# Turning the last query tile's attention probabilities on VectorE and by way of DRAM, for three heads of four, in the first layer

## What is computed

```
h = layernorm(x) * (1 + ca) + sa
q, k, v = h @ q_w, h @ k_w, h @ v_w            # 16 heads of 16 features
scores = q @ k.T / 4 - slope[head] * |i - j|   # per batch and head, 512 x 512
scores = where(j <= i, scores, -inf)
attn = softmax(scores, axis=-1)
x = x + ga * ((attn @ v) @ o_w)
```

## Time and profile before

| | us |
|---|---|
| median of 3 runs | 2975.95 |
| lowest and highest | 2972.04, 2979.3 |
| profiled execution | 2970.31 |
| its span | 2968.5 |
| TensorE, VectorE, ScalarE busy in the span | 2771.0, 1723.5, 1402.0 |

### The profile page before, as it was taken

The page is one execution under the profiler, slowest core; times in us unless marked ns, Lnnn a source line. Parts: engine busy times, 40 slices in busy tenths (PEclk is TensorE's granted clock), DMA queues, the critical chain, the costliest instruction groups (busy, mean ns, idle before and its releaser), DMA issues. The chain is left out here.

```text
span 2968.5 us, 51611 instructions
## 1 busy us (share of the span) xinstructions
PE 2771.0 (93%) x19492; PEld 1833.8 (62%) x19492; DVE 1723.5 (58%) x5077; ACT 1402.0 (47%) x3113; POOL 819.9 (28%) x829
## 2 busy tenths in 40 slices
PE   6889999888799999999999999999999787899998
PEld 3556666664456565656666665656566444478887
DVE  4667777767766565656565555656663688631113
ACT  3666676652445454554545454545442232232224
POOL 1001111113433333323232333333332210035551
PEclk8999999999899999999999999999999899899999
DMA  5111111002554545545555546454441000213325
GB/s 147 19 19 19 19 19 19 14 4 74 169 157 118 155 131 170 160 134 150 146 165 155 158 125 176 122 168 124 143 132 61 11 15 15 71 43 84 76 81 195
DMA packets 218343, 294.19 MB, mean 99 GB/s; under 512 B 23075, under 2 KB 155174, under 8 KB 213984
## 3 DMA queue, kind: packets, MB, share of 16 engines
q1 hardware_dynamic: 209264, 270.37, 31.5%
q0 software_dynamic: 7680, 16.32, 2.1%
q10 hardware_dynamic: 1152, 4.19, 0.4%
HBM read 159.45 MB, written 127.50 MB: 97 GB/s over the span
## 5 line engine op out<-in xcount | busy, mean ns | idle before, releaser
L1576 PE MATMUL bank<-w,gT 128*128 128x256 f32 x2048 | 478.7, 385 | 2.6 <-ACT gT L1494 2.6
L1543 PE MATMUL bank<-h2T,w 128*128 128x512 f32 x1024 | 452.7, 595 | 0.0
L1576 PEld LDWEIGHTS bank<-w,gT 128*128 128x128 f32 x2048 | 379.2, 190 | 90.5 <-issue 44.1
L1494 ACT ACTIVATE gT<-bank,vec 128x512 f32<-128x512 f32 x256 | 175.9, 687 | 425.4 <-PE bank L1543 425.4
L1543 PEld LDWEIGHTS bank<-h2T,w 128*128 128x128 f32 x1024 | 192.1, 190 | 219.6 <-issue 215.2
L609 ACT ACTIVATE y<-y,least 128x128 f32<-128x128 f32 (+3 forms) x512 | 252.0, 554 | 51.5 <-DVE least L479 51.5
L1166 POOL TENSOR_TENSOR prob<-prob,rsum 128x512 f32<-128x512 f32 (+1 forms) x256 | 232.0, 932 | 150.4 <-DVE rsum L1347 150.3
L479 DVE CUSTOM_DVE_ANT_0 y<-bank,mask 128x128 f32<-128x128 f32 (+3 forms) x512 | 223.9, 485 | 71.1 <-PE bank L706 70.2
L1438 ACT ACTIVATE prob<-prob,least 128x256 f32<-128x256 f32 (+1 forms) x512 | 238.2, 466 | 2.2 <-DVE least L1324 2.2
L1324 DVE CUSTOM_DVE_ANT_0 prob<-bank,mask 128x256 f32<-128x256 f32 (+1 forms) x512 | 164.3, 387 | 121.2 <-PE bank L1531 121.2
L1514 PE MATMUL bank<-wtok,hT 128*128 128x512 f32 x512 | 226.5, 595 | 1.3 <-ACT hT L1429 1.3
(11 more groups left out here) (326 smaller groups left out, 4834.6 us busy)
## 6 DMA issues: line engine op xcount, KB each, us to landing
turned_probs<-prob_blocks SPq DMA_DIRECT2D x128, 256.0 KB, 5.5
probT<-turned_probs SPq DMA_DIRECT2D x32, 1024.0 KB, 5.9
turned_rows<-score SPq DMA_DIRECT2D x252, 128.0 KB, 3.1
score<-turned_rows SPq DMA_DIRECT2D x63, 512.0 KB, 3.6
turned_probs<-prob_blocks SPq DMA_DIRECT2D x128, 192.0 KB, 3.1
probT<-turned_probs SPq DMA_DIRECT2D x32, 768.0 KB, 5.0
w<-in_W SPq DMA_DIRECT2D x8, 1024.0 KB, 8.1
turned_queries<-kneg SPq DMA_DIRECT2D x128, 64.0 KB
```

Of the source, the lines that this page charges most:

```text
L1494: nc.scalar.activation(gT[:, m, :], M[m % 2][:, :], ACT.Gelu, bias=vec[:, h // B, 4 * KD + m:4 * KD + m + 1])\
L1543: ins = nc.tensor.matmul(M[m % 2][:, :], w1[:, k, m * P:(m + 1) * P], h2T[:, k, :], start=(k == 0), stop=(k == KD - 1))
L1576: ins = nc.tensor.matmul(M[i][:, (t % 2) * D:(t % 2 + 1) * D], gT[:, m, t * P:(t + 1) * P], w2[:, m, :], start=(m == 0), stop=(m == MF - 1))
```

## The change

```diff
+            def move_wide(m):
+                sp.wait_ge(s["wide_turned"], ROUND * (m + 1))
+                if m:
+                    sp.wait_ge(s["wide_in"], 16 * m)
+                for i in range(GROUPS):
+                    src = blocks[SQUARE * i:SQUARE * (i + 1), :, :, :].rearrange("p a k r -> p a (k r)")
+                    sp.dma_start(c.probs_dram[0][:, :, i, :].rearrange("a p n -> p a n"), src)\
+                      .then_inc(s["wide_away"], 16)
+                sp.wait_ge(s["wide_away"], 16 * GROUPS * (m + 1))
+                if m:
+                    full(sp, ("AV", m - 1, 0))
+                sp.dma_start(wideT.rearrange("p i k r -> p (i k r)"),
+                             c.probs_dram[0].rearrange("a p i n -> (a p) (i n)")).then_inc(s["wide_in"], 16)
+
             for n in range(SLOTS + 2 * QUADS):
                 b, q = divmod(n, QUADS)
+                if 0 <= n - 1 < SLOTS:
+                    move_wide(n - 1)
...
+            def turn_wide(n, heads):
+                for j in heads:
+                    dve.wait_ge(s["exped0"], 4 * n + 1)
+                    if n and j == 0:
+                        dve.wait_ge(s["wide_away"], 16 * GROUPS * n)
+                    nc.vector.transpose(out=blocks[:, :, NT * j:NT * (j + 1), :].rearrange("p a k r -> p k a r"),
+                                        in_=prob[:, j, FROM[3]:FROM[3] + T].rearrange("p (k a f) -> p k a f", a=GROUPS,
+                                                                                      f=SQUARE))\
+                      .then_inc(s["wide_turned"], 1)
...
-                turned(m, (6,))
+                turned(m, (3,))
                 if live:
                     shifted(n, 1, 0, (2, 3))
                     shifted(n, 1, 1, range(4))
+                    turn_wide(n, (0, 1))
                 taken(parts[3])
-                turned(m, (9,))
+                turned(m, (6,))
                 if live:
                     shifted(n, 2, 0, range(4))
+                    turn_wide(n, (2,))
                 taken(parts[4])
...
+                    if tile == 3:
+                        pe.wait_ge(s["wide_in"], 16 * (m + 1))
...
                 work(parts[1])
                 if turns:
-                    turn_probs(m, (4, 5))
+                    turn_probs(m, (4,))
                 work(parts[2])
                 if live:
                     scores(n, 1)
                 if turns:
-                    turn_probs(m, (6, 7, 8))
+                    turn_probs(m, (5, 6))
                 work(parts[3])
                 if turns:
-                    turn_probs(m, (9, 10))
+                    turn_probs(m, (7,))
```

More of the change, by code:

```diff
@@ L125 @@
 FROM = (0, P, 3 * P, 6 * P)
-TURNED = [(3, j, 1) for j in range(4)] + [(2, j, 1) for j in range(4)] + [(0, 0, 4)] + [(1, j, 2) for j in (0, 2)]
-ON_ACT = (1, 3, 5, 7, 8, 10)
+ROUND = 3
+SQUARE = 32
+GROUPS = P // SQUARE
+WIDE = ROUND * NT
+TURNED = [(3, j, 1) for j in range(ROUND, 4)] + [(2, j, 1) for j in range(4)] + [(0, 0, 4)] + [(1, j, 2) for j in (0, 2)]
+ON_ACT = (0, 2, 4, 5, 7)
 PTS = len(TURNED)
@@ L206, in layer0 @@
         rawT = sb("rawT0", [P, QUADS, T])
-        probT = sb("probT0", [P, 4, 1280])
+        probT = sb("probT0", [P, 4 * 1280])
         least = sb("least0", [P, 2, NT, 4])
         den = sb("den0", [P, NT, H0])
-        tmp = sb("tmp0", [P, 2, 2, D])
+        blocks = sb("wide_blocks", [P, GROUPS, WIDE, SQUARE])
         mask = sb("mask0", [P, T])
@@ L283, in evacuate @@
             width = P * (tile + 1)
-            copy(probT[:, j:j + nj, FROM[tile]:FROM[tile] + width],
+            dst = lowT[:, j:j + nj, FROM[tile]:FROM[tile] + width] if tile < 3 else lastT[:, j - ROUND:j - ROUND + nj, :]
+            copy(dst,
                  H[at % 2][:, 0:nj * width].rearrange("p (j n) -> p j n", j=nj))\
@@ L476, in shifted @@
                 for j in heads:
-                    if n:
+                    if n and tile == 3 and j < ROUND:
+                        dve.wait_ge(s["wide_turned"], ROUND * (n - 1) + j + 1)
+                    elif n:
                         dve.wait_ge(s["pt_full0"], PTS * (n - 1) + 1 + turn_of(tile, j))
@@ L568, in _ @@
                 taken(parts[0])
-                turned(m, (2,))
+                turned(m, (1,))
                 if live:
@@ L574, in _ @@
                 taken(parts[1])
-                turned(m, (4,))
                 taken(parts[2])
@@ L666, in _ @@
                 live = n < SLOTS
-                turned(m, (1,))
+                turned(m, (0,))
                 taken(parts[0])
@@ L670, in _ @@
                     exps(n, 0, 0, (0, 1))
-                turned(m, (3,))
+                turned(m, (2,))
                 taken(parts[1])
@@ L674, in _ @@
                     exps(n, 0, 0, (2, 3))
-                turned(m, (5,))
                 taken(parts[2])
@@ L678, in _ @@
                     exps(n, 1, 0, (0, 1))
-                turned(m, (7,))
+                turned(m, (4,))
                 if live:
                     exps(n, 1, 0, (2, 3))
-                turned(m, (8,))
+                turned(m, (5,))
                 taken(parts[3])
@@ L685, in _ @@
                     exps(n, 1, 1, range(4))
-                turned(m, (10,))
+                turned(m, (7,))
                 taken(parts[4])
@@ L881 @@
 CLEARED = 512
-SQUARE = 32
-GROUPS = P // SQUARE
 PROBS = (12, 16)
@@ L1066, in move_queries @@
                 if g:
-                    sp.wait_ge(s["queries_in"], 16 * g)
+                    queries_in.wait(sp, 16 * g)
                     sp.wait_ge(s["linout_full"], g)
@@ L1074, in move_queries @@
                 sp.dma_start(qlT[:, :], c.queries_dram.rearrange("a p i n -> (a p) (i n)"))\
-                  .then_inc(s["queries_in"], 16)
+                  .then_inc(queries_in.sem, 16)
             def move_probs(g, h):
-                sp.wait_ge(s["probs_turned"], 4 * g + 2 * h + 2)
+                probs_turned.wait(sp, 4 * g + 2 * h + 2)
                 if g:
@@ L1653, in _ @@
                 if attn:
-                    pe.wait_ge(s["queries_in"], 16 * (g + 1))
+                    queries_in.wait(pe, 16 * (g + 1))
                     linear_out(g)
```

25 lines of the change are left out of this document (18 added, 7 removed).

## The result

| | before | after |
|---|---|---|
| median | 2973.99 (4 runs) | 3005.36 (4 runs) |
| lowest and highest | 2965.08, 2979.3 | 3003.48, 3009.6 |
| span of the profiled execution | 2968.5 | 3002.8 |
| slots 8 to 27 in it | 383.51 | 409.36 |
| start of the second layer's first product (L107) in it | 702.68 | 741.11 |

The table's times are in us. The ratio is 1.0108, 95% interval 1.0087 to 1.0129: the change makes the kernel 31 us slower. The forecast of 2976 is wrong, and 3005 lies beyond the range's upper end of 3000.

What follows compares the result with a forecast made beforehand. TensorE's work plus two waits for copies per slot bounds the first layer; slots 0.0 x 5 batches and ends gave -3 us, the clock +3, sum 0: median 2976 us, range 2958 to 3000.

Steps and rivals of the forecast that it cites:

- What bounds the kernel now: First layer, 32 slots of four heads (quad q = n % 4): TensorE's work plus two waits for copies sets slot length.
- B: Scores unit 1 to unit 2 in a slot: wait grows from 0.92 to about 1.8 us, 6.14 instead of 6.04.
- A: Scores unit 0 to unit 1 in a slot: -0.23, -0.29, -0.35, -0.50 us for q = 0 to 3.
- C and the three turns: Scores unit 2 to next slot: q = 1 values 1.19 us later, wait 1.57 to about 2.7; other quads unchanged.
- The transfers: Four of 192 KB out and one of 768 KB in: 8.1 us, covered, cost nothing.
- Ends: First and last slots: slot 0 +1.24, slots 1 to 7 -2.0, slots 28 to 31 -0.1, after the last -1.8 us.
- The clock, a cost of its own: TensorE's granted clock: removing turning blocks costs none, longer stretch ahead of q = 1 values; one further low spell, +3 us.
- The slower rival: Clock drops in each of seven q = 1 slots with a 2.7 us wait ahead of the values: 2987 to 3000, chance 0.29.
- the work simply leaves: TensorE 1.39 us a slot shorter throughout the first layer: -43, 2933 us, chance 0.06.
- A pays in full: Copies between scores units 0 and 1 are early enough, B as forecast: -11, 2965 us, chance 0.21.

Runs made afterwards that it cites:

- e10: Changed kernel plus unread products on TensorE, two behind scores unit 1 and two ahead of the q = 1 values, mask waited for only before slot 1; 2967.41 us.
- e1: Changed kernel with VectorE's copy of group 3 ahead of its shifts and ScalarE's copy of group 4 ahead of its exponentials; 2968.17 us, ratio 0.9997.
- e9: Changed kernel, both copies early, q = 1 third turn in the next slot, unread products in remaining waits, mask waited for only before slot 1; 2944.41 us.
- e2: Changed kernel plus two unread products behind scores unit 1, TensorE waiting for the mask tile at its start; 2979.74 us, ratio 1.0033.
- e7: Changed kernel plus two unread products behind scores unit 1 and two ahead of the q = 1 values, mask waited for at TensorE's start; 2971.68 us.
- e11: Changed kernel plus one unread product behind scores unit 1 and two ahead of the q = 1 values, mask waited for only before slot 1; 2964.80 us.
- e4: Kernel before plus the three block turns and five transfers a slot, result unread, TensorE still turning all 40 blocks; 2982.02 us, ratio 1.0039.

## Why the prediction was wrong

**What bounds the kernel now**: right. The waits for copies decided, not the work: twelve blocks less a slot took 0.2 to 0.5 us from A and nothing from B.

**B**: right, to 0.05 us at full clock. Forecast: wait about 1.8, B = 6.14. Measured: 1.73, and B = 6.16 where the clock stayed (slots 14, 18, 22; 6.15 to 6.17 in slots 12 to 27 of e10), q = 0 5.53 for 5.48.

**A**: right. Forecast for q = 0 to 3 8.30, 8.29, 7.34, 7.02; measured 8.31, 8.26, 7.35, 7.04.

**C and the three turns**: right. The values in q = 1 waited 2.54 for about 2.7, C = 6.66 for 6.7; the other quads kept theirs. A turn took 0.694 us on the mean, as the forms of VectorE's lines of the changed kernel say, beside the second layer's 0.704:

```profile
L516 DVE STREAM_TRANSPOSE wide_blocks<-y 128x512 f32<-128x512 f32 x96 | 64.2, 694 | 0.0
```

**The transfers**: right. Their issues in the changed kernel (count, KB each, median us to landing) are as long as those of the earlier trace rows, and nobody waited for them on TensorE. The first line holds 32 issues of each layer:

```profile
probT<-turned_probs SPq DMA_DIRECT2D x64, 768.0 KB, 4.8
...
turned_probs<-wide_blocks SPq DMA_DIRECT2D x128, 192.0 KB, 3.1
```

**Ends**: nearly right. Slot 0 +1.19 for +1.24; behind slot 31 -1.3 for -1.8. Slots 0 to 7 together -2.3 in e10 for -0.8; but the kernel before has a low stretch of 2.7 us in slot 7, so at full clock on both sides they bring about +0.4, and the gain forecast for them is not there.

**The clock, a cost of its own**: this step failed. It took one further low stretch, +3 us; there was one behind scores unit 1 in every slot with odd q from 11 to 27 and in some others, and e10 puts the clock at 38 us, most of it (25.5 us by slots) in B. The working had gone wrong in two ways, and perhaps in a third. It looked for the risk where an old wait grew to 2.7 us, ahead of the values in q = 1, and not in B, where it had itself let a wait grow from 0.92 to 1.8. It used to size two stretches, but not to compare what stood ahead of them with what the change would put ahead of VF: from the end of VF at 471.02 to its next run at 477.06 nothing but blocks through the identity, scores of 17 rows and 0.57 + 1.73 = 2.3 us of waits. And, the third, it took the turning blocks that leave for worth as little to the clock as the waits that come. The kernel before, TensorE in slot 21, the last product ahead of such a stretch, and the first of its two waits:

```profile
442.60 1.89 PE L780 MATMUL bank<-wf,kact 128*128 128x256 f32 x8
...
446.00 0.66 PE L803 MATMUL bank<-ident,rawT 128*128 128x128 f32 x4 [0.42 <-DVE x L528]
```

From its end at 444.49 to VF at 449.93 are 5.44 us of the same kind, with 0.42 + 0.92 = 1.34 us of waits (the 0.92 in the earlier trace rows), and the clock stayed. In slot 23 of the changed kernel it is 4.78 us (512.79 to 517.57) with 1.73 of waits, and it fell. So the shorter stretch fell, with more waiting in it. By the rule that the step cited (the Trainium skill, TensorE: Matmul & The Clock Gate, Part 4: PE-mode transpose: a transpose does not count as TensorE's being busy in the same way) the longer stretch, which had more turning in it, should have been the worse one. Here the trace does not agree: the stretch with more turning and less waiting kept the clock. How much turning counts stays open, for no run changes it alone, and in slot 7 of the kernel before, 8.2 us of the same kind with all its turning and these waits, the clock fell:

```profile
178.07 1.20 PE L722 MATMUL bank<-ident,y 128*128 128x128 f32 x8 [0.92 <-DVE probT L284]
180.16 1.09 PE L722 MATMUL bank<-ident,y 128*128 128x128 f32 x4 [0.90 <-ACT probT L284]
```

**The slower rival** had the mechanism, the clock, and a bound of 3000 us, but its place was only second: behind the values in q = 1 the changed kernel lost some 6 us in all, most of it in slots 5 and 9, and little later (C 6.86 on the mean of slots 12 to 27 for 6.66). Its price, 3.95 - 2.39 = 1.56 us, was paid in full in e1, where the clock had not fallen just ahead of it.

**The rivals that the work simply leaves and that A pays in full**: excluded by B. With the copies early, B does fall to 5.12.

## What to carry to other kernels

When work is taken off the engine that bounds, look at what that engine waits for behind it: here the time went into a wait for a copy that kept its old place in another engine's order, and only with the copies moved ahead and the remaining waits filled did a saving appear (e9). A wait on TensorE is to be priced twice, by its length and by what the matmuls behind it cost at the lower clock, above all where turning, narrow matmuls and waits follow each other without a full product between them; a granted clock of 0.91 in one stage is the line on the page that tells. Products that nobody reads, put into such waits, are a cheap test of that cause and may be worth keeping, if they do not wait for a late operand themselves (5 us at the start in e2 and e7).

## What was not expected of the hardware

- The clock falls for waits of less than 2 us: 1.73 us, with turning and narrow scores around it, brought VF from 1.89 to 3.54 us in slot 21, and B to 7.85 in all eight slots with odd q from 12 to 27. With one product in the wait and 0.67 us left idle it did not fall there (e11).
- The fall is seen behind the wait, not in it: 1.00 in the stretch with the wait, 0.50 from about 1 us after TensorE had started again.
- Added work made the kernel faster: TensorE busy 433 us of 460 in e10 for 390 in the changed kernel, and 38 us less time.
- Four transfers of 192 KB and one of 768 KB in each slot, which raise the DMA share from 0.11 to 0.38, slowed nothing that the traces show: at full clock A, B and C in slots 12 to 27 of e4 are those of before, but for what the three turns add to C in q = 1.
